# Key sums on column halves, spare products that place images in instruction blocks, expert slots in twos

## What is computed

```python
h = concat([patch_tokens(x), txt], axis=1)            # [16, 548, 192]
h = h + performer(layernorm(h))                       # 12 heads of 16, 44 features a head
#   k1 = exp(dash(k) - diag(k) - stab) + eps          [b, h, n, m]
#   kv = einsum('bhnm,bhnd->bhmd', k1, v); ksum = sum(k1, axis=n)
#   out = einsum('bhnm,bhmd->bhnd', q1, kv) / einsum('bhnm,bhm->bhn', q1, ksum)
h = h + gated_attention(layernorm(h))                 # 3 experts of 64, causal, top 2
h = h + talking_heads(layernorm(h))
#   attn = th1 @ (q k^T * scale) + b; attn = softmax(attn); attn = th2 @ attn + b; out = attn @ v
h = h + experts(layernorm(h))                         # 9 experts, 192 -> 768 -> 192
#   route = argmax(softmax(x @ Ws + bs)); p = max(...)
#   where(route == 0, common * scaling, p * chosen + (1 - p) * common), common = expert 0
```

## Time and profile before

| | before |
|---|---|
| median of the runs | 4411.56 us (4411.24 to 4413.79) |
| the profiled execution's own time | 4403.09 us |
| its span, first to last instruction | 4401.3 us |
| PE busy | 4211.0 us, 96% |
| DVE, ACT, POOL busy | 57%, 50%, 39% |
| mean granted TensorE clock | 0.988 |

### The profile page before, as it was taken

The page is one execution under the profiler, slowest core; times in us unless marked ns, Lnnn a source line. Parts: engine busy times, 40 slices in busy tenths (PEclk is TensorE's granted clock), DMA queues, the critical chain, the costliest instruction groups (busy, mean ns, idle before and its releaser), DMA issues. The chain is left out here.

```text
span 4401.3 us, 198101 instructions
## 1 busy us (share of the span) xinstructions
PE 4211.0 (96%) x86686; PEld 3265.8 (74%) x86686; DVE 2527.7 (57%) x7242; ACT 2184.8 (50%) x5035; POOL 1707.9 (39%) x2793
## 2 busy tenths in 40 slices
PE   6999998999989999999999999999999999999998
PEld 4666666767657777777777777777777777899998
DVE  5766886676646655555565556655665554432332
ACT  3443443555536655555555555555555553213444
POOL 2223344767743333333333333333333331001555
PEclk8999998999999999999999999999999999999999
DMA  4112110000000000000000000000000001332333
GB/s 114 24 24 55 40 40 7 1 2 1 1 14 4 16 4 16 23 16 4 15 16 16 4 16 16 16 4 16 16 12 8 16 16 39 75 90 60 64 66 54
DMA packets 122896, 114.53 MB, mean 26 GB/s; under 512 B 64001, under 2 KB 110595, under 8 KB 122043
## 3 DMA queue, kind: packets, MB, share of 16 engines
q1 hardware_dynamic: 94646, 66.47, 6.4%
q0 software_dynamic: 16768, 23.59, 2.9%
q10 hardware_dynamic: 10628, 11.80, 1.2%
HBM read 59.89 MB, written 41.48 MB: 23 GB/s over the span
## 5 line engine op out<-in xcount | busy, mean ns | idle before, releaser
L2254 PE MATMUL PS<-th_kT,th_qg 64*61 64x274 f32 (+1 forms) x21120 | 1440.2, 393 | 9.2 <-issue 6.2
L1949 POOL TENSOR_TENSOR th_qg<-th_qT,w_th_th 128x180 f32<-128x180 f32 x1760 | 849.5, 505 | 1359.2 <-PE PS L2254 1349.1
L2145 ACT ACTIVATE th_P<-PS 119x600 f32<-119x600 f32 x880 | 649.0, 738 | 845.3 <-PE PS L2240 844.9
L2254 PEld LDWEIGHTS PS<-th_kT,th_qg 64*61 64x61 f32 (+1 forms) x21120 | 828.1, 132 | 235.9 <-issue 32.7
L2063 DVE TENSOR_REDUCE th_nmx<-PS 125x1 f32<-125x548 f32 x880 | 639.6, 727 | 622.8 <-PE PS L2254 621.9
L2240 PEld LDWEIGHTS PS<-th_mixn,th_P 61*55 61x55 f32 x35200 | 655.4, 125 | 191.0 <-issue 71.7
L2240 PE MATMUL PS<-th_mixn,th_P 61*55 61x60 f32 x35200 | 688.3, 214 | 52.8 <-issue 44.9
L2155 ACT ACTIVATE th_P<-PS,th_nb 125x548 f32<-125x548 f32 x880 | 622.4, 707 | 109.9 <-DVE th_nb L2066 109.6
L1382 POOL TENSOR_SCALAR ga_P<-ga_P,ga_rw 110x110 f32<-110x110 f32 (+4 forms) x240 | 264.9, 1115 | 160.6 <-DVE ga_rw L1550 159.8
L2279 PE MATMUL PS<-th_P,th_v 119*32 119x90 f32 (+1 forms) x11520 | 253.9, 244 | 7.1 <-issue 6.1
L2066 DVE TENSOR_SCALAR th_nb<-th_nmx,w_th_b 125x1 f32<-125x1 f32 x880 | 240.1, 273 | 32.2
(11 more groups left out here) (366 smaller groups left out, 6351.3 us busy)
## 6 DMA issues: line engine op xcount, KB each, us to landing
pf_xT<-pf_spill SPq DMA_DIRECT2D x32, 412.5 KB, 5.3
ex_tokens<-th_xn SPq DMA_DIRECT2D x124, 82.5 KB
pf_spill<-pf_xT SPq DMA_DIRECT2D x16, 412.5 KB, 3.7
ex_turned<-th_rT SPq DMA_DIRECT2D x16, 412.5 KB, 3.4
ex_x<-ex_turned SPq DMA_DIRECT2D x32, 206.2 KB, 4.1
out_h<-X SPq DMA_DIRECT2D x16, 330.0 KB
ex_w<-in_L_ffn_W ACTq DMA_DIRECT2D x18, 288.0 KB
ex_w<-in_L_ffn_W ACTq DMA_DIRECT2D x8, 576.0 KB
```

Of the source, the lines that this page charges most:

```text
L1949: ins = pool.tensor_tensor(qg[:, m % SB, :, 64 * s:64 * s + HQ].rearrange("p c (h n) -> p c h n", n=QH), qT[:, im % 2, :, at + s * QH:at + ...
L2145: act.activation(P2[:, :, :, at * QT:(at + 1) * QT].rearrange("p t h (s n) -> p s (t h) n", s=2), PS[0:PK, MB:MB + 2, 0:VO].rearrange("p s ...
L2254: ins = pe.matmul(PS[o:w, bank + a, 0:HK], qg[s, p, c, o:w], kT[s, im % 2, c, :], start=c == 0, stop=c == NC - 1)
```

## The change

Three parts, in three functions.

In `performer` every head gets a product of its own: 12 a tile, of 45 stationary columns (44 features and one of ones) and 34 moving ones, placed alternately on columns 0 to 63 and 64 to 127 of the array. The features of a pair of heads therefore lie at 0 and 64, and the mask products of DVE become two copies, ACT's copy to `raw` becomes two, `raw`, `kvo` and `vso` are filled with zeros at the start by POOL, and the query features follow the same layout.

In `talking_heads` PE runs spare products whose results nothing reads: 39 at the start of the stage, 43 ahead of image 1's first tile and 14 ahead of the first tile of every later image.

In `experts` the slots are taken in twos: two turns, two first products, two second products, and ACT's and DVE's instructions in the same order; six buffers for gathered rows instead of four, eight gathers ahead instead of four, and four buffers of the bias instead of two.

```diff
@@ performer
-    PW, HV = 2 * M + 1, HD + 1
-    W34, VW = 2 * HV, 4 * HV
+    PW, HV = 64 + M + 1, HD + 1
+    FR, W34 = 64 + M, 2 * HV
+    HALVES = ((0, 0), (1, 64))
...
-        e = sb("e", [R, RING, PAIRS, PW])
-        v1 = sb("v1", [R, RING, PAIRS, VW])
-        raw = sb("raw", [PW, 2, PAIRS, VW])
-        kvo = sb("kvo", [2 * M, B, PAIRS, W34])
-        vso = sb("vso", [2 * M, B, PAIRS, W34])
+        e = sb("e", [R, RING, H, M + 1])
+        v1 = sb("v1", [R, RING, H, 2, HV])
+        raw = sb("raw", [PW, 2, PAIRS, 2, HV])
+        kvo = sb("kvo", [FR, B, PAIRS, W34])
+        vso = sb("vso", [FR, B, PAIRS, W34])
...
+                for i, a in enumerate((raw, kvo, vso)):
+                    pool.memset(a[:], 0.0).then_inc(filled, 1)
+                    pool.wait_ge(filled, 4 + i)
...
-                        dve.tensor_tensor(kvo[:, b], raw[0:2 * M, b % 2, :, 0:W34],
-                                          own34[:].unsqueeze(1).broadcast_to([2 * M, PAIRS, W34]), ALU.mult).then_inc(kvown, 1)
+                        for a, o in HALVES:
+                            ins = dve.tensor_copy(kvo[o:o + M, b, :, a * HV:(a + 1) * HV], raw[o:o + M, b % 2, :, 0, :])
+                        ins.then_inc(kvown, 1)
...
-                        act.activation(raw[:, b % 2], PS[0:PW, VB + b % 2, 0:PAIRS * VW].rearrange("p (j x) -> p j x", x=VW), ACT.Copy) \
-                           .then_inc(rawc, 1)
+                        for a, o in HALVES:
+                            ins = act.activation(raw[o:o + M + 1, b % 2].rearrange("p j a d -> p (j a d)"),
+                                                 PS[o:o + M + 1, VB + b % 2, 0:PAIRS * W34], ACT.Copy)
+                        ins.then_inc(rawc, 1)
...
                         for j in range(PAIRS):
-                            ins = pe.matmul(PS[0:PW, VB + b % 2, j * VW:(j + 1) * VW], e[0:r, u % RING, j, :], v1[0:r, u % RING, j, :],
-                                            start=t == 0 and j == 0, stop=t == T - 1, skip_group_check=True)
+                            for a, o in HALVES:
+                                h = 2 * j + a
+                                ins = pe.matmul(PS[o:o + M + 1, VB + b % 2, j * W34:(j + 1) * W34], e[0:r, u % RING, h, :],
+                                                v1[0:r, u % RING, h].rearrange("p a d -> p (a d)"),
+                                                start=t == 0 and j == 0, stop=t == T - 1, skip_group_check=True)
@@ talking_heads
+    SPARE = (39, 43, 14)
...
+                def spare(count, p=None):
+                    for i in range(count):
+                        s, a = i % 2, i // 2 % 2
+                        q = slice(64 * s, 64 * s + HQ + 1)
+                        if p is None:
+                            pe.matmul(PS[64 * a:64 * a + 33, 2 * SB - 2 + s, 0:1], ident[q, 0:33], ident[q, 0:1], start=True, stop=True)
+                        else:
+                            pe.matmul(PS[64 * a:64 * a + 33, MB + s, VO:VO + 1], P[q, p, 0, 0:33], mixn[q, p, 0, 0:1], start=True, stop=True)
...
                 stream(5, 2 * SB - 1)
+                spare(SPARE[0])
...
+                        if i == 0 and b:
+                            spare(SPARE[min(b, 2)], p)
@@ experts
-        AHEAD = 4
+        AHEAD, LEAD, BIASES = 6, 8, 4
...
-                    for j in range(NS):
-                        act.wait_ge(xturned, j + 1)
...
-                        if j:
-                            raise_chosen(act, j - 1)
-                    raise_chosen(act, NS - 1)
+                    for g in (0, 1):
+                        for j in pair(g):
+                            take_turned(j)
+                    for g in range(len(PAIRS)):
+                        for j in pair(g):
+                            raise_chosen(act, j)
+                        for j in pair(g + 2):
+                            take_turned(j)
...
-                        if j + AHEAD < NS:
-                            pick(j + AHEAD)
+                        if j + LEAD < NS:
+                            pick(j + LEAD)
...
-                    turn_chosen(0)
-                    turn_chosen(1)
-                    first_product(0)
-                    pe.wait_ge(added, T * B)
-                    for j in range(NS):
-                        if j + 2 < NS:
-                            turn_chosen(j + 2)
-                        if j + 1 < NS:
-                            first_product(j + 1)
-                        second_product(j)
+                    for g in (0, 1):
+                        for j in pair(g):
+                            turn_chosen(j)
+                    for j in pair(0):
+                        first_product(j)
+                        if j == 0:
+                            pe.wait_ge(added, T * B)
+                    for g in range(len(PAIRS)):
+                        for j in pair(g + 2):
+                            turn_chosen(j)
+                        for j in pair(g + 1):
+                            first_product(j)
+                        for j in pair(g):
+                            second_product(j)
```

More of the change, by code:

```diff
@@ L224, in patch_tokens @@
         wT = sb("wT", [C, 2, KC, NC, 2 * PC])
-        own = sb("own", [2 * M, 2])
         projT = sb("projT", [128, KP, D])
@@ L365, in _ @@
                                    base=0, pattern=[[-1, R]], channel_multiplier=1)
-                pool.memset(own[:], 1.0).then_inc(owned, 1)
                 pool.memset(pf.epsrow[:], 0.0).then_inc(owned, 1)
                 pool.memset(pf.eps[:], 1e-4)
[L369 to L375, removed]
+                pool.wait_ge(owned, 1)
+                for o in (0, 64):
+                    pool.affine_select(out=pf.epsrow[:, o:o + M], in_=pf.epsrow[:, o:o + M], compare_op=ALU.not_equal, fill=1e-4,
+                                       base=-o - M, pattern=[[0, M]], channel_multiplier=1)
                 pool.wait_ge(varied, 1)
@@ L983, in raise_queries @@
                     act.wait_ge(qsub, u + 1)
-                    act.activation(f[:, u % 4, :], f[:, u % 4, :], ACT.Exp).then_inc(qexp, 1)
+                    g = f[:, u % 4, :].rearrange("p (h x) -> p h x", x=64)[:, :, 0:M]
+                    act.activation(g, g, ACT.Exp).then_inc(qexp, 1)
                 def features(u):
@@ L1056, in _ @@
                         pe.wait_ge(rawc, b + 1)
-                        pe.matmul(PS[0:2 * M, VB + b % 2, 0:PAIRS * W34], epsrow[:], raw[:, b % 2, :, W34:VW], start=True, stop=True) \
+                        pe.matmul(PS[0:FR, VB + b % 2, 0:PAIRS * HV], epsrow[:], raw[:, b % 2, :, 1, :], start=True, stop=True) \
                           .then_inc(vsum, 1)
@@ L2321, in experts, with pair @@
         NS = SLOT_TILES
+        PAIRS = [range(j, min(j + 2, NS)) for j in range(0, NS, 2)]
+        def pair(g):
+            return PAIRS[g] if 0 <= g < len(PAIRS) else ()
         def sem(name):
@@ L2484, in _ @@
                     pool.wait_ge(kept, 32 * B)
+                    for j in range(AHEAD, LEAD):
+                        pick(j)
                     for j in range(NS):
-                        if j + AHEAD < NS:
-                            pick(j + AHEAD)
+                        if j + LEAD < NS:
+                            pick(j + LEAD)
                         pool.wait_ge(scaled, j + 1)
```

86 lines of the change are left out of this document (45 added, 41 removed).

## The result

The changed kernel takes 0.9919 of the time of before, with an interval of 0.9901 to 0.9938: medians 4375.58 us (4368.28 to 4385.11, 4 runs) and 4412.24 us. That is 36 us less; 47 were forecast. The profiled execution of the changed kernel took 4380.37 us, 22.7 less than the one of before, and by the first product of each stage its gain lies as follows.

A forecast was written before the change was run, and what follows sets the result against it. PE, busy 4211.0 of 4401.3 us, was taken to bound the kernel. Key sums -24, edges -32, spares +6 and slots +3 gave -47, so 4356 us profiled and 4365 as median; range 4340 to 4402.

The forecast's parts named there:

- Key sums, -24: Performer's key pass: key sums on column halves save 24 us in sum, bounds -32 and +9.
- the change of form: Key pass: PE's array changes its division once more per pair of tiles, at 0.11 us a change, +6 us altogether.
- the 4.78 us of the next pair's key products: Key pass: ACT's and DVE's copies cost nothing, being made under these products; 8 us if late by their whole length.
- The 3 us set aside for block edges: Key pass: denser instructions meet block edges, 15 of 25 in gathers at an estimated 0.2 us each, +3 us.
- Rival C: Key pass: column halves do not overlap, so key sums cost 9 us and the total is -14, 4398 us; chance .13.
- Edges, -32 gross and -26 net: Talking heads: spare products shift block edges to better places, gaining 32 us; the spares themselves cost 6.
- rival D: Talking heads: miscounted edges put all images on a bad place alike, +59 there, total +44, 4456 us; chance .06.
- Slots in twos, +3: Chosen experts: taking slots in twos loses 3 us net, from +7, -1.5 and -1.8.
- The delay of the first scatter: Chosen experts: PE's extra turns and first products, with ACT's copies, make the first scatter perhaps 7 us later.
- 15 intervals win 0.1 each: Chosen experts: only the first 15 scatter intervals shorten, by 0.1 us each, 1.5 us in all.
- The bound on the good side, -6: Chosen experts: if the whole scatter chain follows PE at 4.58 us a slot, the part gains 5 to 6 us.
- The eight gathers: Chosen experts: the last 8 slots instead of 4 run without gathers on the scatters' queue, gaining 1.8 us.

The follow-up runs named there:

- e7: Changed kernel with POOL's output-bias additions for the key pass's last two images moved behind the last maximum over partitions: 0.9888 of the time of before.
- e9: Changed kernel with POOL's output-bias additions moved from the key pass to the query pass, one image at a time: 0.9917 of the time of before.
- e6: Changed kernel with 93 spare products instead of 43 ahead of image 1: 1.0065 of the time of before.
- e4: Kernel before with only the chosen experts' slots taken in twos: 0.9985 of the time of before.
- e1: The changed kernel run again, as base for others on the same chip: 0.9917 of the time of before.
- e3: Kernel before with only the key sums on column halves: 0.9956 of the time of before.
- e2: Changed kernel without any spare products: 0.9946 of the time of before.
- e8: Changed kernel with six gathers ahead instead of eight, slots still in twos: 4579.89 us.
- e5: Changed kernel with 78 spare products instead of 14 ahead of images 2 to 15, one whole block more each: 1.0073 of the time of before.

## Why the prediction was right, and where its sizes were off

The direction and the range held, and the measured gain is a quarter smaller than the forecast. That it came so near is partly luck: two parts gained some 6 and 13 us less than forecast, and the third 10 more.

*Key sums, -24: the product was right, a cover was missing.* 48 matmuls were put at 1.05 us and took 1.15, the change of form at 0.11 and took 0.09; a pair came down by 0.74, where 0.83-0.11 = 0.72 was forecast. Over 40 pairs that is 30. The pass gained 16 to 17. What failed is the step that took everything beside PE as hidden under "the 4.78 us of the next pair's key products": it looked at the new copies and memsets, not at POOL's old round of 17 to 18 us an image, which fitted into PE's 18.8 and does not fit into 16.95. e7 and e9 showed it: with the additions moved out of the way, the pass falls to 288.7 and 280.1, which is 27 of the 30 (e9 also takes POOL's additions away from beside DVE, as said above). Of the 13 that are missing, the waits for weighed values are 6.6 and PE's other waits 3; the 144 products behind the longest wait ran at the lower clock in 5.25 us where three times 1.15 was to be had, 1.8 more. The 3 us set aside for block edges were not there: no row of PE in this pass has a gap to "issue". `raw` was counted with 816 columns and has 408 in its new form; the three memsets took 6.1 us for the 6.4 counted. Rival C is refuted: halves that did not overlap would have given 1.90 us. The Trainium skill's rule ("TensorEngine Tiling (Array Packing)", section Instruction Overhead) led to 1.2 us for the 48, and the measured 1.15 stands nearer to that than my 1.05; its warning against dividing a small dimension further did not come true, since the pair still gained 0.74.

*Edges, -32 gross and -26 net: the mechanism right, the size about right for the 14 images that it counted, smaller in the runs.* The count of instructions placed the edges: e6 put all images at a bad place, as rival D has it. e4 and e1, with fetches of 1.065 and 1.071 us, differ by 2403.3-2383.4 = 19.9 us of stage, of which the shift by the key sums' 1,920 instructions has a share (e3 has 2392.9); the runs of e1 and e2 differ by 13. The sum over 14 images left out images 0 and 15: from e2 to e1 the 14 images gain 24.7 us, near the 26, and image 15 with the end of the stage gives 7.5 back. What else was wrong is the picture of a stall with a fixed price at a place. A block takes as long as its work or its fetch, whichever is longer, and the fetch varies from execution to execution by some 6%. That goes some way to explain why images 2 and 3 repeated the edges of the earlier trace rows but not their 145.62 and 146.24 us; not all of it, since image 2 had fetches of 1.104 us and took 148.39, and in the trace of before it had 1.079 and took 145.62. I had read the gain from two images of one execution, which the prediction named as its weakest point.

*Slots in twos, +3: wrong by 10, measured -7.* The delay of the first scatter was right (+6.8 for +7). The step that failed is "15 intervals win 0.1 each": the mean of all 76 intervals falls by 0.12 to 0.19, since PE's slot fell to 4.49 (I had 4.58) and most scatters then wait only for the one before, in the shortest quarter of the intervals 4.31 us or less. The bound on the good side, -6, had assumed 4.58. The eight gathers were counted as 1.8 us at the end only; e8 shows that they carry the whole order.

*The sum.* On the chip of e1 to e4 the traces give -17, -20 and -7, together -44, near the forecast 47, but e1's trace is of its fastest run. The runs give 36, with an interval of 29 to 44.

## What to carry to other kernels

When PE's round gets shorter, compare the new round with every other engine's round at that place, idle "issue" time around its special instructions included, before calling the rest hidden: POOL's 17 us were cheap under 18.8 and the bound under 16.95. Before moving work to where its own engine has time, look at how long the other engines' instructions take beside it: beside an addition of 2.21 us on POOL, one of 0.27 us on DVE lasted 2.09. Where PE runs many short instructions, count them in blocks of 256 and read several executions: the place of the edges was worth 65 us here, and two executions of one program differed by half of that in this stage (2383.4 and 2414.9). An order that runs further ahead needs its loads as far ahead; the same edit with two gathers fewer cost over 200 us.

## What the runs showed of the hardware that was not expected

A block of 256 instructions took PE 4.02 us where its work was done in 1.23 (e5), and no two fetches of blocks begin less than 3.2 us apart in any trace. A maximum over partitions on POOL takes 0.38 us, and in the traces of before and of the changed kernel POOL runs nothing for 5.7 to 7.4 us ahead of it and 6.6 to 7.8 behind it. A DVE instruction of 0.27 us on average took 2.09 beside POOL's addition of 2.21, all 15 times (e9). PE's clock went to its lower level at the end of the changed key pass at 345.5 us, after a wait of 1.61 us and ahead of the one of 4.87, and in e5 for 3.4 or 6.8 us around the start of each of images 2 to 15, where PE ran 156 matmuls of one column and waited 2.03 to 2.79 us.
